# Expert results stored in plain tiles and gathered by token, in place of scatters, in an attention and mixture-of-experts layer on one core

## The chip, the cores and the metric

The kernel runs on one core of one Trainium2 chip. The metric is the device time of one execution in microseconds (us). A core has five engines with a queue each: TensorE (PE; its weight loads are PEld), VectorE (DVE), ScalarE (ACT), GpSimd (POOL) and SyncE (SP). They run side by side and wait for one another by semaphores. SP here issues only DMAs. POOL issues the indirect DMAs, which take a row index for each of 128 rows from SBUF.

## The reference

x is (4, 1024, 256) in float32, 4096 tokens of 256 numbers, and the context is (4, 154, 192) with a mask. Cut to what matters:

```python
def _router(x, gate_w, e_bias):                # 32 experts, 8 groups
    scores = sigmoid(x @ gate_w.T); sc = scores + e_bias
    ...                                        # best 4 groups, in them the best 6 experts
    topk_w = 2.5 * scores[topk_idx] / sum(scores[topk_idx])
def _ffn(x):
    combine = zeros(T, 32).at[arange(T)[:, None], topk_idx].add(topk_w)
    h = relu(einsum('th,eih->tei', x, up_w)) ** 2       # 256 -> 128 per expert
    moe_out = einsum('tei,ehi->th', h * combine[:, :, None], down_w)
    shared = relu(x @ shared_up_w.T) ** 2 @ shared_down_w.T  # 256 -> 512 -> 256
    return moe_out + shared
x = x + tanh(g_xattn[0]) * cross_attention(layernorm(x), ctx_768, mask)   # 8 heads of 64
x = x + tanh(g_ffn[0]) * _ffn(layernorm(x))
```

Each token goes to 6 of 32 experts, so 24,576 rows of 256 numbers go through the experts.

## The kernel before, in words

The 4096 tokens are 32 token tiles of 128, in eight blocks of four. `x_all` holds all of them in SBUF, and what is added to x is added there.

**Attention and routing.** One loop over the 32 tiles does layernorm, cross attention and its projection (L1039, L1089, L1126, L1138 and L1148 are TensorE's lines in it, L493 is a ScalarE copy and L706 a VectorE addition). A block later come the second layernorm and the router (`norm_out`, `router_slots`, `router_weights`; L720 and L844 are VectorE operations of the router). The router gives every token six slot numbers, one per chosen expert: each expert has a region of rows in the DRAM tensor `routed_rows`, and within it tokens stand in order. A row has 276 numbers: 256 of the normalised token, six slot numbers, six gate weights, six target positions and two more. POOL writes the rows there, one indirect DMA of 128 rows per tile and choice (L407, 192 in all). Regions are closed at the token tiles of `SEG_END`, so that row tiles of 128 can be listed by segment: first the rows of all experts for token tiles 0 to 3, then those for 4 to 7, and so on. Tiles may thus also hold rows that belong to nothing; `pad_row` fills the padding.

**Expert loop.** 224 row tiles, taken as 112 pairs, each tile with its own expert. For pair p:

- SP loads two row tiles into a ring of six pairs (`load_rows`, L349), up to six pairs ahead.
- TensorE transposes them (`rows_t`, L1323), and ScalarE copies that to SBUF (`save_rows_t`, L567). Both run two pairs ahead.
- ScalarE copies the tile's up weights (`copy_up`, L580, a register holds the expert), and TensorE projects up (`expert_up`, L1335).
- VectorE squares the relu (`relu_square`, L963 and L965), and TensorE projects down (`expert_down`, L1350).
- The result goes to `y_sb`, a ring of eight, times the gate weight: for even pairs ScalarE (`save_out`, L589), for odd ones VectorE (`save_out`, L972). VectorE gets weights and target positions from the loaded rows, for two pairs at once (`pick_rows`, L949 to L958).
- POOL scatters the two tiles to the DRAM tensor `token_parts` (L429), in which each token has six consecutive rows.

When all six parts of a token tile are sure to be there (`DONE` lists the pair for each segment), ScalarE's queue loads them as one DMA of 768 KB (`load_parts`, L602), at the pairs of `PART_LOAD`, and VectorE adds them to `x_all` (`add_parts`, L980 to L985) some pairs later. SP stores the finished tile (L353). So are tiles 0 to 27 done.

The shared expert of blocks 5 to 7 is spread over the loop: at every fifth pair, from pair 2 on (`SHARED_STEP`), TensorE does one step, `up_late` (L1221) or `down_late` (L1230). VectorE adds the latter to `x_all` (`add_late`, L767). 20 steps fall in the loop and four after it.

**Tail.** After the last pair SP loads the parts of the last four token tiles (L367), TensorE sums four of each six (L1376), VectorE the rest (L1012 to L1017), and ScalarE's queue stores the tiles (L619).

## Time and profile before

| | before |
|---|---|
| median of 3 runs | 989.25 us (986.32 to 990.95) |
| profiled execution, its own time | 983.5 us |
| its span | 981.3 us |
| mean granted TensorE clock | 0.901 of full speed |
| TensorE busy | 785.8 us (80%) |
| TensorE weight loads | 648.5 us (66%) |
| VectorE busy | 507.1 us (52%) |
| ScalarE busy | 414.9 us (42%) |
| GpSimd busy | 486.3 us (50%) |
| DMA moved | 140.52 MB, mean 143 GB/s |

The profile is of one execution, whose own time is 2.2 us above its span. Busy shares are averages over stages with different limits, so the views by stretch say more. "A <- B" in a waits or groups view means that A stood idle until B released it; "remote" is what the profile writes where it finds no releaser, and "issue" is time in which nothing that it shows was waited for. A releaser is inferred from semaphore events.

### The profile page before, as it was taken

To read this page: it belongs to the slowest core of one execution; us is meant where nothing else is said; L and a number is where in the kernel's file an instruction comes from. 1 tells how busy PE (TensorE), PEld (TensorE's weight loads), DVE (VectorE), ACT (ScalarE), POOL (GpSimd) and SP (SyncE) were. 2 spreads that over 40 slices of the span, in tenths; PEclk is the share of its full clock that TensorE was granted. 3 is DMA by queue.
4 is the path that set the end of the run, shared out by engine and by line. 5 is a ranking of instruction groups with operands and counts; after the bars stand their busy time and mean duration, and the time that the engine had idled before them with its cause. 6 is when DMAs were issued, how large, how long until landed. Compare 5 with 4: busy or idle time off the path is not lost.

```text
span 981.3 us, 17489 instructions
## 1 busy us (share of the span) xinstructions
PE 785.8 (80%) x5420; PEld 648.5 (66%) x5420; DVE 507.1 (52%) x1744; ACT 414.9 (42%) x1251; POOL 486.3 (50%) x487
## 2 busy tenths in 40 slices
PE   6899989778786978738828699887887888898877
PEld 5788867666675766625515387776775777776765
DVE  2666656445364645414325034444566666766674
ACT  1465645254353535321411146543554543555530
POOL 1454352627456272770544506665566555666562
PEclk9999998878798988868958799999999989899889
DMA  9700011411212020430612455555687777878655
GB/s 312 225 2 2 1 65 37 160 35 70 70 47 93 25 87 30 174 110 12 241 69 105 144 168 158 170 157 161 213 269 249 233 256 247 258 243 269 220 162 177
DMA packets 77660, 140.52 MB, mean 143 GB/s; under 512 B 13686, under 2 KB 60033, under 8 KB 77056
## 3 DMA queue, kind: packets, MB, share of 16 engines
q1 hardware_dynamic: 50896, 63.26, 21.4%
q0 software_dynamic: 19968, 52.34, 14.4%
q10 hardware_dynamic: 6704, 23.80, 7.7%
q8 instruction: 45, 0.74, 0.3%
q14 instruction: 47, 0.39, 0.1%
HBM read 73.80 MB, written 69.73 MB: 146 GB/s over the span
## 4 chain that ended last, share of the span: by engine, by line
PE 54%; another core or an unknown queue 13%; DVE 10%; issue 10%; ACT 6%; DVEq 4%; DMA 1%; ACTq 0%
PE ps L1335 7%; PE ps L1350 6%; PE ps L1138 6%; PE ps L1200 4%; PE ps L1148 4%; PE ps L1039 4%; PE ps L1089 3%; PE ps L1323 3%; PE ps L1212 3%; PE ps L1126 3%; ACT att L484 2%; DVEq L1000 2%; PE ps L1230 2%; PE ps L1060 1%
## 5 line engine op out<-in xcount | busy, mean ns | idle before, releaser
L429 POOL DMA_INDIRECT token_parts<-hid,place x112 | 113.0, 1009 | 102.8 <-ACT hid L589 55.9
L1350 PE MATMUL ps<-big,att 128*128 x448 | 128.1, 411 | 43.2 <-DVE att L965 27.8
L407 POOL DMA_INDIRECT routed_rows<-x_n,slots x120 | 118.5, 987 | 78.5 <-DVE x_n L742 44.6
L1335 PEld LDWEIGHTS ps<-att 128*128 128x128 f32 x896 | 124.2, 204 | 33.6 <-issue 16.7
L1335 PE MATMUL ps<-att 128*128 128x128 f32 x896 | 128.3, 289 | 15.2 <-ACT att L580 14.4
L567 ACT ACTIVATE att<-ps 128x512 f32<-128x512 f32 x112 | 66.7, 596 | 168.0 <-remote 80.8
L1350 PEld LDWEIGHTS ps<-big,att 128*128 128x128 f32 x448 | 81.5, 203 | 59.4 <-issue 51.9
L1138 PE MATMUL ps<-att,big 128*64 128x128 f32 x1024 | 82.2, 300 | 28.4 <-issue 15.9
L1138 PEld LDWEIGHTS ps<-att,big 128*64 128x64 f32 x1024 | 66.7, 150 | 42.6 <-issue 25.0
L493 ACT ACTIVATE att<-ps 128x512 f32<-128x512 f32 (+1 forms) x96 | 47.5, 535 | 105.4 <-PE ps L1126 50.8
L400 POOL TENSOR_TENSOR att<-att,rsum 128x1232 f32<-128x1232 f32 x14 | 31.4, 2245 | 112.7 <-DVE rsum L697 112.6
L692 DVE TENSOR_REDUCE nmax<-ps 128x3 f32<-128x462 f32 (+1 forms) x96 | 50.5, 574 | 59.9 <-PE ps L1089 35.0
L580 ACT ACTIVATE att<-big 128x256 f32 x224 | 80.5, 412 | 1.1 <-issue 0.7
L1323 PE MATMUL ps<-cst,mid 128*128 128x128 f32 x448 | 71.1, 282 | 1.5 <-issue 1.5
L484 ACT ACTIVATE att<-ps,nmax 128x154 f32<-128x154 f32 x176 | 65.6, 402 | 7.0 <-DVE nmax L692 6.9
L1148 PE MATMUL ps<-hid,big 128*128 128x256 f32 x256 | 67.6, 411 | 0.0
L1089 PE MATMUL ps<-big 64*128 64x154 f32 x512 | 51.5, 323 | 19.4 <-remote 18.6
L1039 PE MATMUL ps<-x1t,hid 128*128 128x128 f32 x512 | 64.1, 276 | 2.4 <-issue 2.4
L1039 PEld LDWEIGHTS ps<-x1t,hid 128*128 128x128 f32 x512 | 62.6, 192 | 4.4 <-issue 2.7
L1089 PEld LDWEIGHTS ps<-big 64*128 64x128 f32 x512 | 47.2, 205 | 23.3 <-remote 20.0
L1323 PEld LDWEIGHTS ps<-cst,mid 128*128 128x128 f32 x448 | 56.1, 148 | 1.8 <-issue 1.7
L407 POOL DMA_INDIRECT routed_rows<-big,slots x48 | 47.2, 982 | 19.8 <-issue 13.7
(238 smaller groups left out, 1431.6 us busy)
## 6 DMA issues: line engine op xcount, KB each, us to landing
mid<-routed_rows SPq DMA_DIRECT2D x224, 138.0 KB
big<-token_parts ACTq DMA_DIRECT2D x19, 768.0 KB
x_n<-token_parts ACTq DMA_DIRECT2D x9, 768.0 KB
routed_rows<-pad_row SPq DMA_DIRECT2D x1, 4416.0 KB
routed_rows<-pad_row SPq DMA_DIRECT2D x32, 138.0 KB
big<-in_x SPq DMA_DIRECT2D x4, 1024.0 KB, 15.7
big<-in_w_moe SPq DMA_DIRECT2D x2, 2048.0 KB
big<-in_w_moe SPq DMA_DIRECT2D x1, 4096.0 KB
```

The source lines that it names most:

```text
L407: nc.gpsimd.indirect_dma_start(rows, bass.IndirectOffsetOnAxis(ap=slots[:, t, k:k + 1], axis=0), normed(t), None).then_inc(s_sca[t // TB % ...
L429: nc.gpsimd.indirect_dma_start(parts, bass.IndirectOffsetOnAxis(ap=place[:, p // 2 % 8, p % 2 * 2 + j:p % 2 * 2 + j + 1], axis=0), y_sb[p ...
L484: ins = A.activation(prob[T % 3][:, h * JP:h * JP + J], ps[:, q, i * J:(i + 1) * J], ACT.Exp, bias=nmax[:, T % 2, h:h + 1], accum_out=esum ...
L567: A.activation(xt[:, p % 2, :], ps[:, p % 2, :], ACT.Copy).then_inc(s_xts, 1)
L580: ins = A.activation(w_up[p % 2][:, j, :], w_exp[:, bass.ds(e, 1), 0:256].rearrange("p a n -> p (a n)"), ACT.Copy)
L1039: ins = M(ps[:, 6, m * P:(m + 1) * P], wq[:, c, m * P:(m + 1) * P], x1t[:, c, :], start=c == 0, stop=c == KC - 1, skip_group_check=True)
L1089: return M(ps[:, q, at:at + J], q_t[r, m, :], k_all[r, m, b * J:(b + 1) * J], start=False, stop=True, skip_group_check=True)
L1138: ins = M(ps[h % 2 * DH:(h % 2 + 1) * DH, 7, h // 2 * P:(h // 2 + 1) * P], v_all[b][:, at:at + DH], prob_t[:, c * P:(c + 1) * P], start=c ...
L1148: ins = M(ps[:, 7, 0:D], att_t[:, m * P:(m + 1) * P], wo[:, m, :], start=m == 0, stop=m == MC - 1, skip_group_check=True)
L1323: ins = nc.tensor.transpose(ps[:, p % 2, j * 256 + c * P:j * 256 + (c + 1) * P], ring[:, p % 6, j, c * P:(c + 1) * P], ident)
L1335: ins = M(ps[:, 2 + p % 2, j * P:(j + 1) * P], w_up[p % 2][:, j, c * P:(c + 1) * P], xt[:, p % 2, j * 256 + c * P:j * 256 + (c + 1) * P], ...
L1350: ins = M(ps[:, 6 + p % 2, j * D:(j + 1) * D], h_t[:, p % 2, j * P:(j + 1) * P], w_exp[:, bass.ds(e, 1), 256:512].rearrange("p a n -> p (a ...
```

## The change

Results of the experts are no longer scattered into token order. Each pair's two tiles are stored as they are, by plain DMAs on SP's queue, into a new DRAM tensor `expert_rows` of 224 tiles. Tiles of different experts follow one another without gaps there, except where row tiles overlap, and the later tile then covers the earlier (`row_y` lists where each one goes). POOL gathers the six rows of each token, for a whole token tile: six indirect DMAs, which read `expert_rows` at the token's slots. VectorE multiplies by the gate weights as it adds.

- Rows have 256 numbers instead of 276. Gate weights stay in SBUF by token (`token_w`). `pick_rows` goes, and `save_out` is a plain copy: one ScalarE activation, or one VectorE copy.
- `expert_rows` is filled with zeros at the start, by one DMA on SP's queue behind the one that fills the padding.
- VectorE turns slots into rows of `expert_rows` (`pack`), a block at each of the pairs 1, 3, ..., 15.
- `SEG_END` gets 2, 4 and 6 in place of 4, so there are 12 segments. With them the last pair that a segment needs is `DONE` = 22, 28, 34, 40, 52, 64, 76, 88, 100, 106, 109 and, for the last, 112.
- SP issues `store_rows(p - 9)` behind `load_rows(p)`.
- POOL issues the gathers of tile t when its segment is stored and tile t - 3 is summed (the ring has three buffers).
- VectorE sums tile t at pair 29 + 17t//5 and the two after it (`SUM_AT`), for tiles 0 to 24; tiles 25 to 31 follow the loop. ScalarE's queue stores the tiles. TensorE does none of the sums.

```diff
-C_EYE, C_IOTA, C_BASE, C_TRI, C_CUM, C_TILE, C_EXP, C_SEG, C_PAD, C_DST = 0, 128, 160, 192, 320, 448, 672, 673, 674, 675
-R_ID, R_W, R_TO, R_BASE, ROW = D, D + TOPK, D + 2 * TOPK, D + 3 * TOPK, D + 3 * TOPK + 2
+C_EYE, C_IOTA, C_BASE, C_TRI, C_CUM, C_TILE, C_EXP, C_SEG, C_BELOW = 0, 128, 160, 192, 320, 448, 672, 673, 674
...
-SEG_END = (4, 8, 12, 16, 20, 24, 28, 30, 31, NT)
+SEG_END = (2, 4, 6, 8, 12, 16, 20, 24, 28, 30, 31, NT)
...
-PART_LOAD = {DONE[g] + 4 + 3 * i: 4 * g + i for g in range(6) for i in range(4)}
-PART_LOAD.update({DONE[6] + 4 + 2 * i: 24 + i for i in range(4)})
+SUM_AT = {29 + 17 * t // 5: t for t in range(25)}
...
+            sp.dma_start(y_rows.rearrange("(t p) d -> p t d", p=P),
+                         pad_row[:].unsqueeze(1).broadcast_to([P, N_TILES, D])).then_inc(s_zf, 16)
...
+            def store_rows(p):
+                if p % 2 == 0:
+                    sp.load(regs_y[p // 2 % 2], row_y[0:1, 2 * p:2 * p + 4])
+                sp.wait_ge(s_ey[p % 2], p // 2 + 1)
+                for j in range(2):
+                    at = sp.snap(regs_y[p // 2 % 2][p % 2 * 2 + j], min_val=0, max_val=(N_TILES - 1) * P)
+                    sp.dma_start(y_rows[bass.ds(at, P), :], y_sb[p % 8][:, j * D:(j + 1) * D]).then_inc(s_ys[p % 8], 16)
+
+            for p in range(N_PAIRS + 9):
+                if p < N_PAIRS:
+                    load_rows(p)
+                if p >= 9:
+                    store_rows(p - 9)
...
-            bound = pool.to_reg(TOPK * N_TOK - 1)
-            for p in range(N_PAIRS):
-                pool.wait_ge(s_ey[p % 2], p // 2 + 1)
-                for j in range(2):
+            def gather(t):
+                if t in (0, *SEG_END):
+                    done = (*DONE, N_PAIRS)[(0, *SEG_END).index(t)]
+                    for i in range(8):
+                        pool.wait_ge(s_ys[i], 32 * -(-(done - i) // 8))
+                if t == 0:
+                    pool.wait_ge(s_dn, 2 * GAP)
+                    pool.wait_ge(s_pack, NBLK)
+                if t >= 3:
+                    pool.wait_ge(s_fin, t - 2)
+                for k in range(TOPK):
                     nc.gpsimd.indirect_dma_start(
-                        parts, bass.IndirectOffsetOnAxis(ap=place[:, p // 2 % 8, p % 2 * 2 + j:p % 2 * 2 + j + 1], axis=0),
-                        y_sb[p % 8][:, j * D:(j + 1) * D], None,
-                        bounds_check=bound, oob_is_err=False).then_inc(s_ys[p % 8], 16)
+                        parts_sb[t % 3][:, k, :], None, y_rows, bass.IndirectOffsetOnAxis(ap=slots[:, t, k:k + 1], axis=0)
+                    ).then_inc(s_pl2[k] if t == NT - 1 else s_pl[t % 3], 16)
...
-                for j in range(2):
-                    ins = A.activation(y_sb[p % 8][:, j * D:(j + 1) * D], ps[:, 6, j * D:(j + 1) * D], ACT.Copy,
-                                       scale=pair_w[:, p // 2 % 8, j, 0:1])
+                A.activation(y_sb[p % 8], ps[:, 6, :], ACT.Copy).then_inc(s_ey[0], 1)
...
+            def pack(b):
+                dve.drain()
+                s = slots[:, TB * b:TB * b + TB, :].rearrange("p t k -> p (t k)")
+                n = TB * TOPK
+                V.scalar_tensor_tensor(after, s.unsqueeze(2).broadcast_to([P, n, NE]), 1.0,
+                                       base_e.unsqueeze(1).broadcast_to([P, n, NE]), ALU.add, ALU.is_ge)
+                dve.drain()
+                V.tensor_tensor(moved, after, shift[:].unsqueeze(1).broadcast_to([P, n, NE]), ALU.mult)
+                dve.drain()
+                V.tensor_reduce(move, moved.rearrange("p (t k) e -> p t k e", t=TB), op=ALU.add, axis=AX_X)
+                dve.drain()
+                V.tensor_tensor(slots[:, TB * b:TB * b + TB, :], slots[:, TB * b:TB * b + TB, :], move, ALU.add).then_inc(s_pack, 1)
...
             def add_parts(t, step):
-                g = parts_sb[t % 3]
-                if step == 0:
-                    dve.wait_ge(s_pl[t % 3], 16 * (t // 3 + 1))
-                    V.tensor_tensor(g[:, 0:3, :], g[:, 0:3, :], g[:, 3:6, :], ALU.add)
...
+                if step == 0 and t < NT - 1:
+                    dve.wait_ge(s_pl[t % 3], 16 * TOPK * (t // 3 + 1))
+                for k in (2 * step, 2 * step + 1):
...
+                    ins = V.scalar_tensor_tensor(x_all[:, t, :], parts_sb[t % 3][:, k, :], token_w[:, t, k:k + 1], x_all[:, t, :],
+                                                 ALU.mult, ALU.add)
...
+                if p % 2 and p // 2 < NBLK:
+                    pack(p // 2)
...
+                    if p - step in SUM_AT:
+                        add_parts(SUM_AT[p - step], step)
             for t in range(NT - TB, NT):
                 add_late(t)
             dve.drain()
...
+            for t in range(len(SUM_AT), NT):
+                for step in range(3):
+                    add_parts(t, step)
...
-            for t in range(N_LAST):
-                pe.wait_ge(s_pl2[t], 16)
-                for k in range(2, TOPK):
-                    ins = M(ps[:, t, 0:D], ident, sums[:, t, k, :], start=k == 2, stop=k == TOPK - 1)
-                ins.then_inc(s_pp, 1)
```

POOL's order from the last row scatters into the expert loop, before (`hid`, `hot`, `picked`, `x_n` and `big` are memory of the ring `y_sb`):

```order
L407 DMA routed_rows<-att,slots 139392x276 x24
L429 DMA token_parts<-hid,place 53248x256 x8
L429 DMA token_parts<-hot,place 53248x256 x2
L429 DMA token_parts<-picked,place 53248x256 x2
L429 DMA token_parts<-x_n,place 53248x256 x2
L429 DMA token_parts<-big,place 53248x256 x2
```

and now (`big` and `x_n` are the three buffers for parts):

```order
L397 DMA routed_rows<-att,slots 139392x256 x24
L426 DMA big<-expert_rows,slots 128x256 x12
L426 DMA x_n<-expert_rows,slots 128x256 x6
L426 DMA big<-expert_rows,slots 128x256 x12
L426 DMA x_n<-expert_rows,slots 128x256 x6
```

A pair's two scatters became, for each token tile, six gathers in a row.

VectorE in the loop, where a token tile is being summed, before (two pairs):

```order
L963 TENSOR_SCALAR hot<-ps 128x256
L965 SCALAR_TENSOR_TENSOR att<-ps,hot 128x256
L972 TENSOR_TENSOR hid<-ps,pair_w 128x512
L985 TENSOR_TENSOR x_all<-x_all,big 128x256
L963 TENSOR_SCALAR x_n<-ps 128x256
L965 SCALAR_TENSOR_TENSOR att<-ps,x_n 128x256
L949 TENSOR_TENSOR is_e<-mid,tile_key 128x24
L951 TENSOR_TENSOR to_spill<-mid,x_n 128x4
L953 TENSOR_TENSOR pick<-mid,is_e 128x48
L956 TENSOR_REDUCE pair_w<-pick 128x8
L958 TENSOR_TENSOR place<-pair_w,to_spill 128x4
```

and now (three pairs):

```order
L941 TENSOR_SCALAR x_n<-ps 128x256
L943 SCALAR_TENSOR_TENSOR att<-ps,x_n 128x256
L957 SCALAR_TENSOR_TENSOR x_all<-big,token_w,x_all 128x256 x2
L941 TENSOR_SCALAR hot<-ps 128x256
L943 SCALAR_TENSOR_TENSOR att<-ps,hot 128x256
L949 COPY picked<-ps 128x512
L957 SCALAR_TENSOR_TENSOR x_all<-big,token_w,x_all 128x256 x2
L941 TENSOR_SCALAR x_n<-ps 128x256
L943 SCALAR_TENSOR_TENSOR att<-ps,x_n 128x256
L957 SCALAR_TENSOR_TENSOR x_all<-big,token_w,x_all 128x256 x2
```

The picking of weights and positions is gone, and a sum is three steps of two multiply-adds.

VectorE after the last saved result, now (before, the first row was followed by three additions for each of four tiles):

```order
L751 SCALAR_TENSOR_TENSOR x_all<-ps,tanh_g,x_all 128x256 x4
L957 SCALAR_TENSOR_TENSOR x_all<-big,token_w,x_all 128x256 x6
L957 SCALAR_TENSOR_TENSOR x_all<-x_n,token_w,x_all 128x256 x6
L957 SCALAR_TENSOR_TENSOR x_all<-big,token_w,x_all 128x256 x12
L957 SCALAR_TENSOR_TENSOR x_all<-x_n,token_w,x_all 128x256 x6
L957 SCALAR_TENSOR_TENSOR x_all<-big,token_w,x_all 128x256 x12
```

Seven token tiles are summed behind the loop, where it was four.

## Rows read from the trace of the kernel before

**Rows 1.** Busy time by stretch: window, length, busy us of each engine (instructions).

```profile
core 0: us, PE busy (x) PEld busy (x) DVE busy (x) ACT busy (x) POOL busy (x), PEclk, DMA share, GB/s
0.00:583.50 583.50, 453.83 (x3460) 364.03 (x3461) 272.56 (x1053) 228.75 (x783) 258.98 (x263) 0.88 0.27 95
583.50:957.90 374.40, 315.78 (x1897) 271.88 (x1898) 223.80 (x667) 186.10 (x469) 222.88 (x221) 0.94 0.69 216
957.90:981.30 23.40, 16.20 (x64) 12.63 (x63) 10.78 (x25) 0.00 (x0) 4.42 (x4) 0.93 0.55 186
28.00:40.00 12.00, 11.39 (x107) 10.97 (x106) 7.38 (x26) 3.26 (x10) 3.25 (x5) 1.00 1.10 334
425.00:445.00 20.00, 7.27 (x40) 4.51 (x41) 1.04 (x3) 3.43 (x13) 13.54 (x15) 0.50 0.29 106
```

**Rows 2.** Chain of waits in the loop: start us, us, what ran.

```profile
586.40 0.87 PE ps L1350 x4
...
588.60 0.87 PE ps L1350 x4
...
652.42 1.73 PE ps L1230 x8
```

**Rows 3.** Waits of 583.5 to 957.9: waiter, releaser, us, times, mean us.

```profile
ACT att L567 <- remote: 80.8, 22, 5.7
...
POOL token_parts L429 <- issue: 54.8, 179, 0.6
```

**Rows 4.** Timeline, 636 to 646 us: start, us, engine, instruction [idle <- releaser].

```profile
636.77 0.98 POOL L429 DMA_INDIRECT token_parts<-big,place  x1 [1.99 <-DVE big L972]
...
639.54 1.05 PE L1335 MATMUL ps<-att 128*128 128x128 f32 x8
...
640.43 0.60 PE L1323 MATMUL ps<-cst,mid 128*128 128x128 f32 x4
...
643.34 0.99 POOL L429 DMA_INDIRECT token_parts<-hid,place  x1 [0.30 <-issue]
...
645.48 0.60 ACT L567 ACTIVATE att<-ps 128x512 f32<-128x512 f32 x1 [5.30 <-remote]
```

**Rows 5.** Timeline, 431 to 438 us, in the attention part.

```profile
431.39 0.43 DVE L706 TENSOR_TENSOR x_all<-ps,x_all 128x256 f32<-128x256 f32 x1 [9.64 <-remote]
...
436.36 0.60 ACT L493 ACTIVATE att<-ps 128x512 f32<-128x512 f32 x1 [8.24 <-remote]
```

**Rows 6.** Timeline of SP's queue: start us, time over which it issued.

```profile
168.46 0.34 SPq L323 DMA_DIRECT2D big<-in_w_moe  x1
...
646.13 1.96 SPq L349 DMA_DIRECT2D mid<-routed_rows  x4
...
905.23 11.15 SPq L349 DMA_DIRECT2D mid<-routed_rows  x6
```

**Rows 7.** VectorE's groups, 395 to 583 us: busy us, mean ns | idle ahead.

```profile
L844 DVE TENSOR_TENSOR hot<-key,best 128x768 f32<-128x768 f32 x3 | 2.9, 951 | 0.0
```

**Rows 8.** VectorE's groups in the loop, 583.5 to 957.9 us.

```profile
L965 DVE SCALAR_TENSOR_TENSOR att<-ps,hot 128x256 f32<-128x256 f32 x56 | 23.8, 425 | 4.2
...
L963 DVE TENSOR_SCALAR hot<-ps 128x256 f32<-128x256 f32 x56 | 23.7, 424 | 40.6 <-remote 21.5 <-PE ps L1335 15.6 <-issue 1.5
...
L972 DVE TENSOR_TENSOR hid<-ps,pair_w 128x512 f32<-128x512 f32 x28 | 19.2, 686 | 9.7 <-PE ps L1350 7.2 <-remote 1.2 <-issue 1.1
L980 DVE TENSOR_TENSOR big<-big 128x768 f32<-128x768 f32 x18 | 17.1, 950 | 0.1
...
L985 DVE TENSOR_TENSOR x_all<-x_all,big 128x256 f32<-128x256 f32 x18 | 7.5, 417 | 0.0
```

**Rows 9.** Timeline of the tail, 956 to 981 us.

```profile
957.92 8.90 SPq L367 DMA_DIRECT2D big<-token_parts  x4
...
962.20 1.03 POOL L429 DMA_INDIRECT token_parts<-big,place  x1 [0.30 <-issue]
...
971.79 0.48 DVE L767 SCALAR_TENSOR_TENSOR x_all<-ps,tanh_g,x_all 128x256 f32<-128x256 f32 x1 [2.09 <-PE ps L1230]
...
978.70 0.42 DVE L1017 TENSOR_TENSOR x_all<-ps,x_all 128x256 f32<-128x256 f32 x1 [0.47 <-PE ps L1376]
```

More of the change, by code:

```diff
@@ L265, in flamingo_block @@
         s_zf = sem("padding_cleared")
+        s_pack = sem("slots_packed")
         s_ld = [sem(f"rows_loaded_{i}") for i in range(6)]
@@ L328, in _ @@
             regs = [[sp.alloc_register(f"sp_row_{i}_{j}") for j in range(4)] for i in range(4)]
+            regs_y = [[sp.alloc_register(f"sp_result_row_{i}_{j}") for j in range(4)] for i in range(2)]
             for q in range(NE // 4):
@@ L379, in _ @@
             nc.gpsimd.memset(pad_row[:], 0.0)
-            for r in range(3):
-                nc.gpsimd.memset(norm_sets[r][:, :, R_BASE:ROW], 0.0)
             nc.gpsimd.memset(run[:], 0.0)
@@ L614, in _ @@
                     hidden_late(GAP + SHARED_STEP[p] // 8, SHARED_STEP[p] % 8)
-                if p in PART_LOAD:
-                    load_parts(PART_LOAD[p])
-            for t in range(NT - N_LAST, NT):
-                act.wait_ge(s_fin, t + 1)
-                act.dma_start(out_tiles[t], x_all[:, t, :]).then_inc(s_st, 16)
+                if p - 4 in SUM_AT:
+                    store(SUM_AT[p - 4])
+            for t in range(len([at for at in SUM_AT if at + 4 <= N_PAIRS]), NT):
+                store(t)
         @block.vector
@@ L1301, in _ @@
                 M(ps[:, 5, 0:N_TILES], skip_m[0:n, a * P:(a + 1) * P], inside[0:n, a, 0:N_TILES], start=a == 0,
+                  stop=a == NTAB - 1, skip_group_check=True)
+            for a, (_, n) in enumerate(TABLES):
+                M(ps[0:2, 4, 128:128 + N_TILES], skip_y2[0:n, a, :], inside[0:n, a, 0:N_TILES], start=a == 0,
                   stop=a == NTAB - 1, skip_group_check=True)
```

176 lines of the change are left out of this document (53 added, 123 removed).

## The prediction, on record before the changed kernel ran

> **What bounds the kernel now.** I read the busy time by stretch first. It cuts the span into the part ahead of the expert loop (583.5 us), the loop over 112 pairs of expert tiles (374.4 us) and the tail (23.4 us) [rows 1]. The change rewrites the loop's outlet and the tail, so these two are examined.
>
> In the loop I asked what a pair must cost. In the chain of waits, where nothing disturbs it, one down projection (L1350) follows the last by 588.60 - 586.40 = 2.20 us, all of it TensorE work; a late shared step (L1230) costs 1.73 us [rows 2], and 20 of these lie in the loop. So TensorE alone asks for 112 x 2.20 + 20 x 1.73 = 281 us. The loop takes 374.4: 93 us are stalls.
>
> Their cause is the main finding. In the waits of the loop ScalarE's copy L567 stands 80.8 us for something the profile calls remote, and 179 of POOL's 224 scatters start straight behind another ("issue"), so that 224 - 179 = 45 runs of about five remain [rows 3]. The timeline puts the two together [rows 4]: a run of six scatters lasts from 636.77 to 644.32. The transposes that the copy needs were done at 641.03, ScalarE is idle, and the copy starts at 645.48, 1.2 us after the last scatter. TensorE runs on, but its completions arrive only when POOL pauses. In a longer run, in the attention part, it is worse: from 425 to 445 us TensorE is busy 7.27 of 20 us, at a granted clock of 0.50 (the lower level, 1.2 GHz) [rows 1], ScalarE waits 8.24 and VectorE 9.64 us for results [rows 5]. I read: **after some 5 us of indirect DMAs without a pause, completions of TensorE are held until POOL pauses.** In the loop this limits itself, since a held TensorE gives POOL nothing to scatter; a run of six then costs 93 x 6 / 224 = 2.5 us.
>
> The Trainium skill speaks against this reading. Its page "SBUF — State Buffer", section "SBUF: two separate sides", says that engine ports and DMA ports cannot contend. By that rule the 93 us would not follow POOL, and rival A below is what it makes of the change. The trace does not agree here: the held copy of [rows 4] had its operand and an idle engine.
>
> **The change, part by part.**
>
> *Fill of the result rows.* 28,672 rows of 1 KB, 29.4 MB, on SP's queue. The present fill shows the rate: 334 GB/s between 28 and 40 us, TensorE meanwhile busy 11.39 of 12 us at clock 1.00 [rows 1]. So it takes 88 us, over by about 130 us, when that queue has nothing due (w_moe is issued at 168.46 [rows 6]) and the first row scatters are about to start. Cost 0; if it ran longer it would delay w_moe, which is needed 400 us later. Rows shrink from 276 to 256 elements: at most 7% of loads that are hidden six pairs deep. 0.
>
> *Tables.* Some small VectorE operations more and some fewer ahead of the loop: about 1 us either way, 0.
>
> *Pairs 0 to 21.* POOL has nothing to do until 22 pairs are stored. Today it starts at pair 4, so about 18 pairs lose their stalls: 18 x 0.83 (93/112) = 15 us gained. This is inside the count of runs below. Slot packing adds on VectorE, in eight of the first 16 pairs, two operations and a reduction over 768 elements, each like L844 at 0.95 us [rows 7], with a small one about 3 us. With relu (0.42 + 0.43 per pair, 0.93 with its drain, by my estimate) and the saved half (0.69) [rows 8] that is 1.86 + 0.69 + 3.0 = 5.5 us for two pairs against TensorE's 5.0. 8 x 0.5 = 4 us lost.
>
> *VectorE in the sums.* pick_rows goes, five small operations per two pairs. The sum of a token tile was one operation of 0.95 (L980) and three of 0.42 (L985) [rows 8]; it becomes six of 0.43 that each wait for the one before, about 3.0 us per 3.4 pairs. Per pair 0.93 + 0.35 + 0.88 = 2.2 us, under TensorE's 2.20 + 0.31 = 2.5. Hidden, with little to spare; without cover it would cost at most the 0.9. ScalarE drops one of two activations in a save: it isn't the bound, 0.
>
> *SP.* Two plain stores per pair are added to the two loads, and each pair's stores wait in order for the saved result, with later loads queued behind. The loads are issued six pairs ahead, so a wait of a pair or so is hidden. But SP's rate is not free: four DMAs in 1.96 us where POOL mostly pauses (0.49 each), six in 11.15 us beside scatters (1.9, waits included) [rows 6]. Four per pair ask for 2.0 us at best; at twice the bare issue, 1.0 each, for 4.0. Range 0 to +40 us; I take +8, near the lower end, since POOL pauses give SP time and the store itself needs no wait.
>
> *POOL.* 224 scatters become 192 gathers, six per token tile. No trace here shows a gather; nearest is the scatter at 0.98 + 0.30 us, so 7.74 us per tile. Upper bound of their effect on TensorE: as scatters; lower: none. I take the upper, because the held completions appear with scatters of two different kinds (L407, L429) and end with POOL's issue. In the loop, tile t may be gathered when its segment is stored and tile t-3 is summed. Following these two conditions pair by pair, some 158 gathers (26.4 tiles) fall in the loop, in 21 runs: mostly of six, but twelve for tiles 0 and 1 and up to eighteen where a segment of four opens after a wait (tile 8 on). 21 runs at 2.5 us are 52 us. The 32 gathers by which longer runs exceed six find TensorE already held: 32 x 1.29 = 41 us, or 0.7 of it if as much leaks through as in 425 to 445 us. I take 38. Stalls 90 us, against 93 today. The loop: 281 + 4 + 8 + 90 = **383 us**, +8 to +9.
>
> *Tail.* Today 23.4 us: rest of the scatters to 963.23, last load of parts issued by 957.92 + 8.90 = 966.82, the last late shared add at 972.27, four sums that TensorE helps with, last at 979.12, end 981.3 [rows 9]. Now 192 - 158 = 34 gathers are still to issue, one after the other: 34 x 1.29 = 44 us. Then the landing, by the nearest row at most 966.82 - 963.23 = 3.6 us (the load waits for the landed scatter), the last sum 0.5, the store 2.2. Together 50 us, **+27 us**. The late shared steps lie beside it.
>
> Sum: 583.5 + 383 + 50 = 1016.5, against 981.3; with the 2.2 us around the span 1018.7. The profiled execution (983.5) is 5.75 us under the median of the runs (989.25), so I forecast **1024 us**, +3.5%. Its own range, by the bounds above, is 1000 to 1047.
>
> **The rivals.**
>
> *A. Gathers hold nothing up (faster).* Against it: [rows 4, 5]. For it: the direction of the data is reversed. The page named above gives no such effect either. Then the loop is 281 + 4 + about 12 us of waits at segment starts = 297, the tail stays 50: 583.5 + 297 + 50 + 2.2 + 5.75 = 938 us. Range 930 to 960. It decides if a run of six costs under 0.5 us.
>
> *B. Half the stalls.* Runs of six just reach the length at which holding starts, and the first 22 pairs are clean. Stalls 45 to 60 us in place of 90: 583.5 + 281 + 4 + 8 + 50 + 50 + 8 = 984 us, between 960 and 1000: gain in the loop and loss in the tail cancel.
>
> *C. SP becomes the bound.* If each of its DMAs takes 1.0 us beside gathers in 90 pairs, the loop is 22 x 2.6 + 90 x 4.0 = 417 us and the total 1058. For it: [rows 6]. Against: POOL pauses about a third of the time.
>
> **Chances.** Forecast 0.45; A 0.25; B 0.20, of which 0.12 is faster by more than 0.5%, 0.06 within and 0.02 slower; C 0.10. Half a per cent, 5 us, is about what a measurement of this kernel can tell from no change. Faster 0.37, same 0.06, slower 0.57. Cases of both signs hold most of the chance, so the full range runs from A to C: 934 to 1060; the forecast's own is above.
>
> **What would show it.** Right: no POOL work until pair 22 and pairs of 2.5 to 2.8 us there; gathers of about 1.3 us; ScalarE's row copy and VectorE's relu still waiting until runs of gathers end; more than 30 gathers after the last down projection and a tail near 50 us. Wrong: loop near 300 us with ScalarE's waits gone (A), or SP busy issuing all the time and TensorE waiting for rows (C). If gathers take clearly over or under 1.3 us, the tail goes with them.

## The result: 9% slower, 2.7 times the forecast step, and the profile after

The changed kernel took 1083.73 us (median of 4 runs, 1079.9 to 1094.16) against 990.04 us: ratio 1.0916, interval 1.0845 to 1.0988. The forecast was 1024 us within 934 to 1060: the right side, but +35 us (on the 989.25 us of that time) where it was +94. The same kernel, measured again (x5), gave 1.094 (1.0864 to 1.1016). Ratios leave out executions more than 1.5% above the fastest of their kernel; medians and ranges are of all.

The experiments added something that the numbers can't be understood without. They ran in groups, each on one chip together with the kernel before. In this measurement and the first two groups the kernel before takes 974 to 990 us. In the last three groups, on three further chips, it takes 749 to 751 us, and the change 801.16 us (800.1 to 804.67), ratio 1.070 (1.0637 to 1.0762). Below, the first are called **holding chips** and the others **free chips**; every ratio here is between runs of one group.

The profile after is that of x5, whose execution lies at the median. The one taken with the measurement itself is of its longest execution, 1094.16 us (loop 431 us, tail 61 us), and it is the one that the expectations of x1 to x4 speak of. Busy time by stretch, columns as in [rows 1]; ahead of the loop, loop, tail:

```profile
0.00:591.10 591.10, 457.61 (x3460) 369.18 (x3461) 270.36 (x1038) 226.65 (x779) 258.05 (x260) 0.87 0.40 139
591.10:1018.80 427.70, 321.79 (x1906) 278.21 (x1905) 222.59 (x468) 177.82 (x416) 151.94 (x160) 0.87 0.63 189
1018.80:1081.40 62.60, 12.69 (x32) 8.44 (x30) 23.93 (x49) 0.00 (x0) 31.03 (x33) 0.56 0.32 96
```

These stretches, and all that follow, are cut at the first transposes of the loop. [rows 1] cuts 2.3 us later, at the first up projection (583.5). Cut like the others, the kernel before has:

```profile
0.00:581.20 581.20, 452.76 (x3452) 363.21 (x3453) 271.08 (x1047) 227.30 (x779) 258.98 (x263) 0.88 0.27 95
581.20:957.90 376.70, 316.85 (x1906) 272.69 (x1905) 225.28 (x673) 187.56 (x472) 222.88 (x221) 0.94 0.69 215
```

So the loop grew from 376.7 to 427.7 us, the tail from 23.4 to 62.6. TensorE's busy time in the loop is nearly the same (321.79 against 316.85): it waits more. The waits of the loop, which answer to [rows 3] (L566 is the row copy that was L567, L941 the relu that was L963, L1317 the down projection that was L1350):

```profile
POOL big L426 <- issue: 141.7, 99, 97.0
ACT att L566 <- remote: 112.9, 17, 18.7
...
DVE hot L941 <- remote: 71.1, 10, 14.3
POOL x_n L426 <- DVE x_all L957: 58.5, 5, 21.5
PE ps L1317 <- DVE att L943: 52.2, 19, 12.3
```

ScalarE's row copy waits 112.9 us in 17 places where it was 80.8 in 22: fewer, longer holds. POOL waits 58.5 us in five places for VectorE's sums, which free the buffers. The first run of gathers, the timeline that answers to [rows 4]:

```profile
661.93 0.97 POOL L426 DMA_INDIRECT big<-expert_rows,slots  x1 [97.03 <-issue]
...
665.33 1.05 PE L1302 MATMUL ps<-att 128*128 128x128 f32 x8
...
674.12 0.27 PE L1302 MATMUL ps<-att 128*128 128x128 f32 x1 [1.06 <-issue]
...
675.73 0.94 POOL L426 DMA_INDIRECT big<-expert_rows,slots  x1 [0.30 <-issue]
...
679.15 0.42 DVE L941 TENSOR_SCALAR x_n<-ps 128x256 f32<-128x256 f32 x1 [5.03 <-remote]
679.21 0.60 ACT L566 ACTIVATE att<-ps 128x512 f32<-128x512 f32 x1 [9.34 <-remote]
```

POOL is idle for 97 us, until pair 22. Then it issues twelve gathers from 661.93 to 676.67, and ScalarE, idle for 9.34 us, starts 2.5 us behind the last. A gather's cadence is 1.25 us (0.95 + 0.30). Here it isn't only completions that are late: the next eight matmuls of L1302, which took 1.05 us from 665.33 on, come out as five from 670.01 on and three single ones up to 674.39, with idle gaps between them for which the profile shows nothing. The tail, answering to [rows 9]:

```profile
1017.64 1.13 PE L1317 MATMUL ps<-big,att 128*128 x4 [1.44 <-issue]
...
1027.91 0.94 POOL L426 DMA_INDIRECT big<-expert_rows,slots  x1 [0.30 <-issue]
1029.93 0.48 DVE L751 SCALAR_TENSOR_TENSOR x_all<-ps,tanh_g,x_all 128x256 f32<-128x256 f32 x1 [7.33 <-remote]
...
1038.65 0.48 DVE L751 SCALAR_TENSOR_TENSOR x_all<-ps,tanh_g,x_all 128x256 f32<-128x256 f32 x1 [3.88 <-PE ps L1193]
1039.23 3.28 DVE L957 SCALAR_TENSOR_TENSOR x_all<-big,token_w,x_all 128x256 f32<-128x256 f32 x6
...
1043.31 1.16 POOL L426 DMA_INDIRECT big<-expert_rows,slots  x1 [14.46 <-DVE x_all L957]
...
1072.59 1.15 POOL L426 DMA_INDIRECT big<-expert_rows,slots  x1 [0.30 <-issue]
```

The last four late steps are held by gathers (7.33 us), then run on a TensorE at little over half its clock (0.56 in the tail). The sum of tile 25 stands behind them on VectorE, and POOL waits 14.46 us for its buffer. 24 more gathers follow, 30 us, and the end.

### The profile page after: what moved, and what is told of

Its sections match the earlier page's. It is cut to its first block, busy times and chain, and to the rows that moved or that the text cites. A ratio compares the mean times of both kernels' runs of the same rounds, so it can differ in the third digit from the quotient of the medians.

```text
span 1092.3 us, 17615 instructions
## 1 busy us (share of the span) xinstructions
PE 788.1 (72%) x5396; PEld 654.1 (60%) x5396; DVE 517.0 (47%) x1555; ACT 404.7 (37%) x1195; POOL 441.0 (40%) x452
## 4 chain that ended last, share of the span: by engine, by line
PE 45%; another core or an unknown queue 22%; DVE 12%; issue 7%; ACT 5%; DVEq 3%; POOL 2%; DMA 2%; ACTq 1%; POOLq 0%
PE ps L1317 6%; PE ps L1101 6%; PE ps L1302 5%; PE ps L1163 4%; PE ps L1111 4%; PE ps L1002 3%; PE ps L1052 3%; PE ps L1175 3%; PE ps L1089 3%; PE ps L1290 2%; PE ps L1193 2%; DVE x_all L957 2%; ACT att L483 2%; DVE att L943 2%
## 5 line engine op out<-in xcount | busy, mean ns | idle before, releaser
L426 POOL DMA_INDIRECT big<-expert_rows,slots x132 | 126.6, 959 | 237.2 <-issue 148.9
L1317 PE MATMUL ps<-big,att 128*128 x448 | 133.1, 424 | 79.0 <-DVE att L943 64.4
L1302 PEld LDWEIGHTS ps<-att 128*128 128x128 f32 x896 | 128.3, 208 | 34.3 <-issue 23.9
L566 ACT ACTIVATE att<-ps 128x512 f32<-128x512 f32 x112 | 66.7, 596 | 206.2 <-remote 112.9
L1302 PE MATMUL ps<-att 128*128 128x128 f32 x896 | 130.4, 292 | 16.9 <-issue 9.0
L1317 PEld LDWEIGHTS ps<-big,att 128*128 128x128 f32 x448 | 85.0, 211 | 95.2 <-issue 87.0
L1052 PE MATMUL ps<-big 64*128 64x154 f32 x512 | 56.9, 343 | 58.5 <-remote 56.3
L1101 PE MATMUL ps<-att,big 128*64 128x128 f32 x1024 | 78.2, 300 | 22.3 <-ACT att L492 8.6
L426 POOL DMA_INDIRECT x_n<-expert_rows,slots x60 | 57.4, 957 | 89.3 <-DVE x_all L957 55.4
L1052 PEld LDWEIGHTS ps<-big 64*128 64x128 f32 x512 | 50.7, 218 | 63.8 <-remote 59.0
L957 DVE SCALAR_TENSOR_TENSOR x_all<-big,token_w,x_all 128x256 f32<-128x256 f32 x132 | 63.5, 481 | 16.0 <-DMA big<-expert_rows,slots 9.3
L941 DVE TENSOR_SCALAR hot<-ps 128x256 f32<-128x256 f32 x56 | 23.7, 423 | 97.5 <-remote 75.2
```

The costliest lines, as they stand in the source:

```text
L426: nc.gpsimd.indirect_dma_start(parts_sb[t % 3][:, k, :], None, y_rows, bass.IndirectOffsetOnAxis(ap=slots[:, t, k:k + 1], axis=0)).then_in ...
L566: A.activation(xt[:, p % 2, :], ps[:, p % 2, :], ACT.Copy).then_inc(s_xts, 1)
L957: ins = V.scalar_tensor_tensor(x_all[:, t, :], parts_sb[t % 3][:, k, :], token_w[:, t, k:k + 1], x_all[:, t, :], ALU.mult, ALU.add)
L1052: return M(ps[:, q, at:at + J], q_t[r, m, :], k_all[r, m, b * J:(b + 1) * J], start=False, stop=True, skip_group_check=True)
L1101: ins = M(ps[h % 2 * DH:(h % 2 + 1) * DH, 7, h // 2 * P:(h // 2 + 1) * P], v_all[b][:, at:at + DH], prob_t[:, c * P:(c + 1) * P], start=c ...
L1302: ins = M(ps[:, 2 + p % 2, j * P:(j + 1) * P], w_up[p % 2][:, j, c * P:(c + 1) * P], xt[:, p % 2, j * 256 + c * P:j * 256 + (c + 1) * P], ...
```

## The experiments

**First group, on a holding chip.** Theory 1 is the forecast's: a run of indirect DMAs (a string of them without a pause of POOL) holds TensorE's completions, and its length decides.

**x1, plain loads for the gathers.**

```diff
-                    nc.gpsimd.indirect_dma_start(parts_sb[t % 3][:, k, :], None, y_rows, bass.IndirectOffsetOnAxis(...))
+                    nc.gpsimd.dma_start(parts_sb[t % 3][:, k, :], x_tiles[:, (t + 5 * k) % NT, :])
...
```

> The changed kernel, but each gather is a plain load of the same 128 KB, from the input x, issued by POOL at the same place and with the same waits (so the sums get rows that are not the experts' results). Theory 1, long runs of indirect DMAs hold TensorE's completions: the stalls of ScalarE's row copy and VectorE's relu go, the loop falls from 431 to 300-320 us and the tail from 61 to 30-45 us, in all 930 to 960 us. Theory 2, the added stores and the load on SP's queue are what slows the loop: the loop stays above 400 us, the total above 1040 us.

Median 935.04 us; ratio 0.954 (0.9478 to 0.9598). Its loop, POOL's issue of the plain loads, and what the row copy (here L565) waits for in the loop:

```profile
594.20:902.20 308.00, 289.21 (x1907) 259.58 (x1906) 223.25 (x468) 179.78 (x416) 85.71 (x162) 0.98 0.82 263
```

```profile
L426 POOL DMA_DIRECT2D big<-in_x x132 | 69.9, 541 | 185.4 <-DMA expert_rows<-picked 95.7 <-DVE x_all L956 50.6 <-DMA expert_rows<-big 26.7
```

```profile
ACT att L565 <- PE ps L1289: 110.9, 98, 11.3
```

Theory 1 hits. In this one execution waits on "remote" stand ahead of the loop, where the row scatters are still indirect (57.9 us on one ScalarE copy alone), and none stands in the loop. The stores, the fill, the sums and 263 GB/s leave the loop at 308 us, so theory 2 (the forecast's rival C) falls: SP can't have cost more than a part of 308 - 2.3 - 281 = 25 us. One thing x1 doesn't separate: its loads also follow closer together. A run of twelve takes 6.45 us (665.42 to 671.87), where twelve gathers take 14.7. Whether a string of plain loads of 15 us would hold TensorE too wasn't tested.

**x2, runs of six.** `GATHER_AT` lists for the first 28 tiles the pair from which each may start, three pairs apart.

```diff
...
+                if t < 28:
+                    pool.wait_ge(s_edn, GATHER_AT[t] + 1)
                 for k in range(TOPK):
```

> The changed kernel, but POOL issues a token tile's six gathers only from a pair of their own on (three pairs from tile to tile), so that runs of 12 and 18 become runs of six with a pause. The same 192 gathers are issued. Theory 1 (what a run costs grows with its length beyond about five): the loop falls by 35 to 60 us, from 431 to 370-395 us. Rival, each gather costs TensorE the same wherever it stands: the loop stays within 10 us of 431.

1040.09 us, ratio 1.071 (1.0668 to 1.0753). The loop:

```profile
586.30:972.70 386.40, 317.23 (x1907) 274.77 (x1906) 222.68 (x468) 176.56 (x416) 154.03 (x160) 0.92 0.70 210
```

As many gathers fall in the loop (POOL, x160), and it takes 386.4 us, though three of the runs still have twelve. x3, on the same chip, has the change's own loop, untouched, and takes 415.0; so some 29 us are gained there, a little under what was expected (41 against x5's 427.7, on another chip). What the gathers cost depends on how they are strung.

**x3, order of the tail.**

```diff
+            for t in range(len(SUM_AT), NT - TB):
+                for step in range(3):
+                    add_parts(t, step)
             for t in range(NT - TB, NT):
                 add_late(t)
             dve.drain()
-            for t in range(len(SUM_AT), NT):
+            for t in range(NT - TB, NT):
                 for step in range(3):
                     add_parts(t, step)
```

> The changed kernel, but behind the loop VectorE sums token tiles 25 to 27 before it adds the last four late shared steps. Theory: the 12 us for which POOL waited for the sum of tile 25, which stood behind four late steps held by gathers, goes: 8 to 13 us faster than the change. Rival: the late steps are then held by the longer run of gathers and end last: no gain, within 3 us.

1063.76 us (1046.47 to 1073.31) against 973.92. The time decides nothing: the executions spread over 27 us, all four give 1.092, which is the change's own ratio, and the two fastest (1057.58 and 1046.47 us) give 1.079. The stretches and the timeline show what happened:

```profile
582.80:997.80 415.00, 323.02 (x1906) 279.82 (x1905) 222.53 (x468) 177.71 (x416) 152.56 (x160) 0.88 0.65 195
997.80:1055.70 57.90, 13.12 (x33) 8.79 (x31) 23.94 (x49) 0.00 (x0) 31.23 (x33) 0.57 0.35 104
1030.57 0.48 DVE L751 SCALAR_TENSOR_TENSOR x_all<-ps,tanh_g,x_all 128x256 f32<-128x256 f32 x1 [12.21 <-remote]
```

The rival's mechanism is there: the last run became 30 gathers without a pause, and the late steps were held by it instead; the last of them is added 38 us behind the loop, where it was 20. POOL's wait for a buffer fell only from 14.46 to 9.66 us, and the tail from 62.6 to 57.9.

**x4, the fill alone in the kernel before.**

```diff
+            fill = nc.dram_tensor("extra_rows", [N_TILES * P, D], F32, kind="Internal").ap()
+            sp.dma_start(fill.rearrange("(t p) d -> p t d", p=P),
+                         pad_row[:, 0:D].unsqueeze(1).broadcast_to([P, N_TILES, D])).then_inc(s_zf, 16)
...
```

> The kernel before with the change's fill alone: 29.4 MB of zeros written to an unused DRAM tensor, at the same place of SP's queue. Theory, the fill is hidden and the 17 us that the change's part ahead of the loop took more are row scatters that ran together in longer runs: within 4 us of the kernel before. Rival, the fill itself costs them: 10 to 17 us slower than the kernel before.

975.68 us, ratio 0.9998 (0.9959 to 1.0037). The fill costs nothing that the measurement can tell.

**Second group, on another holding chip.** x5 is the change as it is:

> The changed kernel as it is, once more, as the measure for the runs beside it. Its ratio to the kernel before was 1.092; expected 1.08 to 1.10. If the part ahead of the loop takes 580 to 587 us in this profile, where it was 600 us in the first, that difference is spread between executions and no effect of the change.

1083.61 us, ratio 1.094. The part ahead of the loop took 591 us, between what the two cases named. In seven profiles of the change and its variants on holding chips it is 583 to 601 us, in three of the kernel before and its variants 581 to 587. Whether the change costs something there, some 10 us at most by these, stays open; on the free chips it is 429 against 430.

**x6, a quarter of the bytes.**

```diff
-                        parts_sb[t % 3][:, k, :], None, y_rows, ...
+                        parts_sb[t % 3][:, k, 0:64], None, w_moe.rearrange("p e (n d) -> (p e n) d", d=64), ...
```

> The changed kernel, but each gather brings 64 of 256 columns (from the input with the expert weights; the sums thus get other numbers): the same count of indirect DMAs and of rows, a quarter of their bytes. Theory 1a, it is POOL's issue of indirect DMAs that holds TensorE's completions: the loop stays within 12 us of the change's, 415 to 431 us. Rival 1b, it is the bytes that they move: the loop falls below 350 us.

1078.53 us, ratio 1.0898 (1.0807 to 1.0989), loop 423.4 us: 1a. POOL's time for a gather doesn't change either:

```profile
L426 POOL DMA_INDIRECT big<-in_w_moe,slots x132 | 126.2, 956 | 243.0 <-issue 134.0 <-DVE x_all L957 46.2 <-DMA expert_rows<-hid 32.2
```

**x7, two gathers per pair.** As x2, with the wait ahead of each two gathers, at `GATHER_AT[t] + k // 2`.

> The changed kernel, but two gathers per pair, each two behind a wait for that pair's down projection (from pair 22 on, later where the segment asks). Theory: POOL pauses itself when TensorE's completions are late, runs stay under six, and the loop is 340 to 370 us where it was 386 with runs of six. Rival: held completions come in one lot, runs of six form again, as in the kernel before: 375 to 390 us.

1038.68 us, ratio 1.0516 (1.044 to 1.0591), loop 374.9 us, which is the rival's end. In the timeline the runs have 2 to 12 gathers, eight of them eight or more (a pause under 0.75 us isn't counted as one, here and below): as the timeline reads, what was held arrives for several pairs at once, and the waits of several pairs are over together.

**x8, longer runs in the kernel before.**

```diff
             for p in range(N_PAIRS):
-                pool.wait_ge(s_ey[p % 2], p // 2 + 1)
+                last = min(p // 6 * 6 + 5, N_PAIRS - 1)
+                if p % 6 == 0:
+                    pool.wait_ge(s_ey[last % 2], last // 2 + 1)
+                    pool.wait_ge(s_ey[(last - 1) % 2], (last - 1) // 2 + 1)
```

> The kernel before, but POOL scatters six pairs at once, so its runs have 12 scatters where they had six; nothing else changes. Theory 1: TensorE runs for some 5 us of each run of 15.5 us and then is held; a cycle of six pairs takes about 25 us, the loop 440 to 480 us in place of 375. Rival, only gathers get dearer with the length of a run, or a scatter costs the same wherever it stands: the loop stays under 395 us.

1093.3 us, ratio 1.1057 (1.0986 to 1.1128). The loop, and one of its runs (L570 is the row copy, L1326 its transposes):

```profile
586.60:1060.10 473.50, 346.15 (x1906) 294.49 (x1905) 227.33 (x673) 190.29 (x472) 211.47 (x211) 0.82 0.54 170
```

```profile
709.64 0.98 POOL L432 DMA_INDIRECT token_parts<-hid,place  x1 [11.88 <-DVE picked L975]
...
713.21 0.60 ACT L570 ACTIVATE att<-ps 128x512 f32<-128x512 f32 x1 [1.27 <-PE ps L1326]
...
717.67 0.87 PE L1326 MATMUL ps<-cst,mid 128*128 128x128 f32 x4
...
723.82 0.98 POOL L432 DMA_INDIRECT token_parts<-picked,place  x1 [0.30 <-issue]
726.92 0.60 ACT L570 ACTIVATE att<-ps 128x512 f32<-128x512 f32 x1 [12.50 <-remote]
```

473.5 us, where it was 376.7. A cycle of six pairs takes 26 us (17 of them from 606.35 to 1051.02). The run's length alone, with scatters and with nothing of the change, costs more than the change does: long runs of scatters hold as runs of gathers do.

**Third group, on a free chip: pauses.** Four kernels in which POOL clears a small buffer between indirect DMAs: in x9 five times ahead of every fourth gather, as here; in x10 with the late steps in the loop too; in x11 and x12, made from the kernel before, four times ahead of every second pair's scatters and twice ahead of each pair's.

```diff
-SUM_AT = {29 + 17 * t // 5: t for t in range(25)}
+SUM_AT = {30 + 19 * t // 5: t for t in range(21)}
...
+                    sent = TOPK * t + k
+                    if sent % 4 == 0:
+                        for _ in range(5):
+                            nc.gpsimd.memset(pad_row[:], 0.0)
+                            pool.drain()
```

> The changed kernel, but POOL clears a small buffer five times (some 2 us) ahead of every fourth gather, whatever the other engines do; since POOL is slower so, token tiles are summed from pair 30 on every 3.8 pairs, 21 of them in the loop. Theory: a run of four gathers (5.0 us) is over before completions are held, so the stalls nearly vanish: ScalarE's row copy waits under 40 us for nothing that the profile shows (113 before), the loop falls from 428 to 310-345 us, some 60 gathers are left behind it, and the end is set by POOL: 970 to 1010 us. Rival: completions are held while POOL is busy with anything: loop 430 us or more.

> As the run with the pauses, and the last four late shared steps stand in the loop (one step in 4.5 pairs in place of 5). Theory: the loop gains their 4 x 1.7 = 7 us and the end stays where POOL sets it, within 5 us of the run with the pauses. Rival: the late steps were in the way of the last sums: 8 to 15 us faster than that run.

> The kernel before, with a pause of some 1.6 us on POOL ahead of every second pair's scatters, so that a run has four scatters (5.2 us) at most. Theory: stalls nearly vanish, POOL's own rate sets the loop: 56 x (5.2 + 1.6) = 380 us at worst, and 345 to 365 us where POOL's pauses replace those that it had: 10 to 30 us faster than before. Rival: the time that POOL loses is added: loop 395 us or more.

> The kernel before, with a pause of some 0.8 us on POOL ahead of each pair's two scatters. Theory: if a short pause is enough to release what is held, the loop is POOL's 112 x (2.6 + 0.8) = 380 us at most, and 345 to 370 us. Rival, a pause of 0.8 us releases nothing: 385 to 420 us.

981.01, 985.02, 995.51 and 1084.32 us, against 750.66 us: ratios 1.307, 1.311, 1.326 and 1.446. x9 and x10 fall in or near the numbers foretold, and that means nothing: the chip held nothing, and the pause was not what it was meant to be. POOL in x9:

```profile
509.89 0.33 POOL L429 MEMSET pad_row<- 128x256 f32 x1
512.99 1.60 POOL L429 MEMSET pad_row<- 128x256 f32 x4 [2.77 <-issue]
515.37 0.95 POOL L431 DMA_INDIRECT big<-expert_rows,slots  x1 [0.78 <-issue]
```

The first drain behind gathers takes 2.8 us or more, so a pause is 5 us instead of 2 and POOL's own rate, four gathers in 10 us, sets the end. The four runs tell nothing on theory 1.

**Fourth group, on a free chip.** x17 is the change as it is. (x13 to x16, the same four kernels, were never executed and gave no numbers.) In x18 the pause is four clears of four buffers, without a drain; x19 adds the four late steps to the loop; x20 is the kernel before with that pause.

```diff
-SUM_AT = {29 + 17 * t // 5: t for t in range(25)}
+SUM_AT = {30 + 37 * t // 10: t for t in range(22)}
...
+                    n = TOPK * t + k
+                    if n % 4 == 0:
+                        if n:
+                            pool.wait_ge(s_idle, n // 4)
+                        nc.gpsimd.memset(x1t[:], 0.0)
+                        nc.gpsimd.memset(pad_row[:], 0.0)
+                        nc.gpsimd.memset(skip_m[:], 0.0)
+                        nc.gpsimd.memset(run[:], 0.0).then_inc(s_idle, 1)
```

> The changed kernel as it is. Where the kernel before takes 970 to 990 us: 1.085 to 1.10 of it. Where it takes 750 us and nothing is held: the loop is set by TensorE's 281 us with small waits, the tail by 32 gathers, so the change costs the tail's 30 to 37 us alone, ratio 1.02 to 1.06.

> The changed kernel, but POOL clears four small buffers (1.4 us, some 2 us from gather to gather) ahead of every fourth gather, with no drain; token tiles are summed from pair 30 on every 3.7 pairs, 22 of them in the loop. Where completions are held by long runs: theory, runs of four are over before the hold, the loop is 310 to 350 us (428 as changed), POOL sets the end at 583 + 67 + 48 x 6.7 + 7 = 979 us, spread 965 to 1000: ratio 0.98 to 1.01. Rival, POOL's clearing counts as work of the same kind and nothing is released: loop above 430 us. Where nothing is held: slower than the change by the pauses' time, up to 60 us.

> As the run with the pause without a drain, with the last four late shared steps in the loop. Theory, POOL sets the end: within 5 us of that run. Rival, late steps are in the way of the last sums: 8 to 15 us faster than it.

> The kernel before with the same pause ahead of every second pair's four scatters. Where long runs hold completions: the loop is POOL's 56 x 7.1 = 398 us at most; 375 to 400 us, so the same or up to 20 us slower, since the pauses come on top of those that POOL has. Where nothing is held: 40 to 70 us slower than the kernel before.

x17: 801.16 us, ratio 1.070, above the 1.02 to 1.06 that were expected. x18: 822.91 us, 1.099 (1.0929 to 1.1051). x19: 819.33 us, 1.093 (1.0875 to 1.0989), 3.6 us under x18, as if POOL sets the end. x20: 812.6 us, 1.085 (1.079 to 1.0907), 64 us slower than before. x18 to x20 came as foretold for a chip that holds nothing; whether a pause of 2 us releases anything on one that does was not seen. x17's stretches and one of its waits in the loop:

```profile
0.00:429.20 429.20, 402.74 (x3460) 333.74 (x3461) 269.12 (x1038) 225.03 (x779) 266.67 (x260) 0.99 0.55 190
429.20:745.30 316.10, 289.75 (x1907) 260.76 (x1906) 223.66 (x468) 180.15 (x416) 149.75 (x156) 0.97 0.84 256
745.30:799.30 54.00, 7.84 (x33) 5.62 (x31) 23.95 (x49) 0.00 (x0) 35.35 (x37) 0.61 0.41 124
```

```profile
584.53 0.95 POOL L426 DMA_INDIRECT x_n<-expert_rows,slots  x1 [16.42 <-DMA expert_rows<-hid]
...
595.07 1.05 DVE L957 SCALAR_TENSOR_TENSOR x_all<-x_n,token_w,x_all 128x256 f32<-128x256 f32 x2 [12.91 <-DMA x_n<-expert_rows,slots]
```

POOL stands idle for 16.42 us for the segment of tiles 8 to 11, and VectorE, whose sum of tile 8 stands at a fixed pair, waits 12.91 us for it with the next relu queued behind. x1 shows the same wait on a holding chip: 10.21 us for the plain loads of that tile. POOL's runs in x17's loop are long, four of 12 and four of 24 gathers, and then one of 48 that reaches into the tail.

**Fifth group, on a free chip.** x21 is the kernel before, for its profile; x22 the change with shorter segments.

```diff
-SEG_END = (2, 4, 6, 8, 12, 16, 20, 24, 28, 30, 31, NT)
-SUM_AT = {29 + 17 * t // 5: t for t in range(25)}
+SEG_END = tuple(range(2, NT + 1, 2))
+SUM_AT = {28 + 3 * t: t for t in range(28)}
```

> The kernel before as it is, for its profile. Where it takes 750 us and nothing is held: part ahead of the loop 428 us, loop 293 to 303 us (POOL's 224 scatters ask for 289), tail 19 to 27 us; single waits of ScalarE's row copy of 5 us and more on nothing that the profile shows are gone. Where it takes 970 to 990 us: as in the first profile, loop 370 to 380 us.

> The changed kernel with 16 segments of two token tiles in place of 12, and the sum of tile t at pair 28 + 3t, 28 of them in the loop. Where nothing is held: POOL no longer stands idle for some 35 us between segments, so 18 to 22 gathers are left behind the loop instead of 36, the loop falls from 316 to 298-308 us and the tail from 54 to 32-38 us: 25 to 40 us faster than the change, ratio to the kernel before 1.015 to 1.035. Rival: the tail is set by something else than the gathers that are left: within 10 us of the change. Where completions are held: loop within 15 us of 428, tail 15 to 20 us shorter, ratio 1.06 to 1.09.

x21: 750.19 us, ratio 1.0009, and its stretches, with one of 45.8 us in which POOL issued 36 scatters in a row:

```profile
0.00:430.20 430.20, 403.27 (x3453) 333.75 (x3454) 269.87 (x1047) 225.05 (x779) 267.35 (x263) 0.98 0.37 127
430.20:725.10 294.90, 286.14 (x1906) 257.60 (x1905) 226.85 (x674) 192.06 (x472) 221.34 (x215) 0.99 0.85 276
725.10:752.30 27.20, 20.62 (x64) 15.46 (x63) 10.74 (x24) 0.00 (x0) 9.03 (x9) 0.74 0.49 160
```

```profile
339.30:385.10 45.80, 45.02 (x229) 29.57 (x225) 25.00 (x131) 17.97 (x32) 35.11 (x36) 1.00 0.56 204
```

TensorE is busy for 45.02 of those 45.8 us at full clock; the stretch from 425 to 445 us of [rows 1] had 7.27 of 20. ScalarE's row copy stands idle 88.5 us, of which 75.2 on TensorE, and none on "remote", which no waits view of a free chip's profile has:

```profile
L567 ACT ACTIVATE att<-ps 128x512 f32<-128x512 f32 x112 | 66.9, 597 | 88.5 <-PE ps L1323 75.2 <-DVE x_all L985 4.5 <-issue 4.3
```

In the loop it is now POOL that sets the pace. From this scatter on, its 220 scatters follow one another without a pause of even half a microsecond, to 736.82 us:

```profile
443.67 0.98 POOL L429 DMA_INDIRECT token_parts<-hid,place  x1 [1.23 <-ACT hid L589]
```

x22: 781.47 us, ratio 1.042 (1.039 to 1.0449). By the ratios, 1.070 and 1.042, some 21 us are gained on the change, less than was expected:

```profile
430.00:748.60 318.60, 291.19 (x1906) 258.98 (x1905) 232.50 (x488) 180.33 (x416) 167.86 (x174) 0.99 0.86 263
748.60:779.40 30.80, 7.89 (x33) 5.64 (x31) 14.30 (x29) 0.00 (x0) 17.73 (x19) 0.74 0.41 123
```

```profile
DVE x_all L957 <- DMA big<-expert_rows,slots: 22.9, 13, 4.4
...
DVE x_all L957 <- DMA x_n<-expert_rows,slots: 10.9, 8, 3.6
```

The tail fell to 30.8 us, with some 18 gathers in it. The loop did not fall: with a sum every three pairs VectorE now waits 33.8 us in 21 small pieces of the loop for gathers. No version made here is faster than the kernel before, on either kind of chip.

## Why the forecast was right on the side and wrong on the size

By stretches, in us, all cut at the first transposes of the loop (the kernel before from its own profile and x21, the change from x5 and x17):

| | before, holding | change, holding | before, free | change, free |
|---|---|---|---|---|
| ahead of the loop | 581.2 | 591.1 | 430.2 | 429.2 |
| loop | 376.7 | 427.7 | 294.9 | 316.1 |
| tail | 23.4 | 62.6 | 27.2 | 54.0 |

Against the terms of the forecast, on its own cut (2.3 us later), the profiled execution (1081.4 us) is 64.9 us longer than its 1016.5: 9.9 ahead of the loop (593.4 for 583.5), 42.4 in the loop (425.4 for 383) and 12.6 in the tail (62.6 for 50).

**The finding on held completions** was right for the chip that it was read from: x1, x2, x6 and x8 show there that the stalls come with indirect DMAs, follow the length of their runs and not their bytes. That it is completions alone that are held is a reading of [rows 4]; in x5's first run TensorE's own instructions were late too. Told as a rule of the hardware it is wrong: on a free chip 220 scatters in a row hold nothing. The forecast had no case for a chip without it. On the loop before it is worth 376.7 - 294.9 = 82 us, where the forecast took all 93 us above TensorE's own need for stalls of this kind. The rule of the Trainium skill's page "SBUF — State Buffer", section "SBUF: two separate sides", that the forecast weighed against the trace agrees with the free chips (TensorE busy for 45.02 of 45.8 us beside 36 scatters), and no run here shows which path holds TensorE on the others.

**The failed step is the count of runs in the part on POOL**: "158 gathers ... in 21 runs: mostly of six", with 32 gathers beyond six. The number in the loop was right (160). But x5's timeline has them in 18 runs, six of 12 and two of 18, so 60 beyond six (the last run reaches into the tail); with two pauses of 0.73 and 0.64 us counted as pauses it is 20 runs and 48 beyond six. With the forecast's own prices, 18 x 2.5 + 60 x 1.29 = 122 us of stalls come out, or 20 x 2.5 + 48 x 1.29 = 112, in place of 90. Measured, the loop of the change is 427.7 - 316.1 = 112 us longer on the holding chip than on the free one. The price of a run thus stood up, the string of runs did not.

The forecast had a twelve for tiles 0 and 1 and eighteens from tile 8 on. It missed the twelves for tiles 2 and 3 and for 16 and 17, both at the opening of a segment, the one for 26 and 27, for which POOL had waited 12.66 us for a sum of VectorE, and, where so short a pause isn't counted, those for 21 and 22 and for 24 and 25. That the holds themselves delay the sums, and so lengthen the next run, fits this but isn't shown; on the free chip, where nothing is held, the same conditions string up runs of 12 and 24.

**The loop without any hold** is the second term that was mis-sized: 4 (packing) + 8 (SP) = 12 us were forecast beside the stalls, and 316.1 - 2.3 - 281 = 33 us stand in the loop on a free chip. Packing was right: from the first transposes to the 23rd down projection the change takes 66.8 us and x21 61.9. SP's 8 us can't be told apart. Missing was a wait that the change adds: a sum at a fixed pair, on the engine that serves the loop, waits for gathers whose segment has only just opened (12.91 us at tile 8). The forecast called the sums hidden, since it priced their work and not what they wait for.

**The tail** was forecast at 50 us and measured at 62.6. The gathers left behind were right (34 forecast, 32 measured), and so was their pace (1.29 against 1.25). Wrong was "the late shared steps lie beside it": they stand ahead of the sums on VectorE, and POOL waited 14.46 us for the sum behind them. On a free chip, where nothing holds them, POOL doesn't wait there; the tail is 54.0 us and its growth, 54.0 - 27.2, the forecast's +27, which is in part luck, since some 36 gathers were left behind that loop and the tail before was longer too.

**Ahead of the loop** the forecast said 0. The fill is 0 (x4). The 9.9 us of this profile stay open: profiles of one kernel differ by as much there (591 and 601 for the change).

**The rivals.** A (gathers hold nothing) fell on holding chips. On free chips its premise holds, and the change is still 7% slower: A's gain came from stalls that would vanish, and there are none to vanish. Its price of 938 us was met by x1, 935 us, where plain loads stand for gathers, but by luck: in x1's profile, on the forecast's cut, the loop is 9 us and the part ahead of it 13 us longer than A's terms, and the tail 14 us shorter. B and C fell. The doubt that would have helped, that more runs come out longer than six, has no case: the range of the stalls moves only the price of the 32 gathers (0.7 to 1.0), never their number.

## What to carry to other kernels

Where a stall is tied to runs of one kind of instruction, what a change does to the length of the runs counts more than how many instructions it saves: on a holding chip 192 gathers, many strung in twelves and eighteens, cost more than 224 scatters, most of them in sixes. Work that waits for a transfer doesn't belong at a fixed place in the queue of the engine that feeds the critical loop, and work that frees a buffer shouldn't stand behind work that others don't wait for (this second point is read from the timeline of the tail; x3, which moved that work, gained nothing that stood out of its spread). Before a stall is taken for a rule, it should be seen on more than one chip: here a quarter of the time, 240 us, hung on which chip ran it.

## What was not expected of the hardware

- The same kernel takes 974 to 990 us on some chips and 749 to 751 us on others (granted clock 0.90 and 0.99). In the first, what TensorE completes reaches other engines late in runs of indirect DMAs; in the second, 220 scatters in a row (x21, 443.67 to 736.82 us) hold nothing. What differs in the chips is open.
- A drain on POOL behind four gathers and a small clear takes 2.8 us and more (x9: 2.77 and 4.06 us of idle time ahead of the next clear).
- POOL spends 0.956 us on a gather of 128 rows, be they 1 KB or 256 B (x5: 955 ns, x6: 956 ns), and 0.541 us on a plain load of 128 rows (x1). The plain loads, twelve in 6.45 us while TensorE had work, held nothing on a holding chip.
